# A decoder's second cross attention: steps of two key tiles and sums of exponentials on GpSimd

## The reference, cut to what matters

```
q = x @ Wq ; k = context @ Wk ; v = context @ Wv        # per head 1024x64, 6404x64, 6404x64
p = exp(q @ k.T / 8 - max)                              # softmax over the 6404 keys
o = (p @ v) / p.sum(-1)
y = x + concat(o) @ Wo + bo ; then a layer norm
```

## Time and profile before

| | us |
|---|---|
| median of 3 runs (lowest, highest) | 5546.07 (5544.38, 5546.73) |
| span of the profiled execution | 5512.1 |
| its own time beside the span | the runs' median is 34.0 above the span |
| busy: TensorE, VectorE, ScalarE, GpSimd | 4651.9, 3773.2, 2570.0, 866.4 |
| second cross attention, first K item to the last Y | about 2800 to 5386 |

### The profile page before, as it was taken

How to read it: one execution, slowest core, us unless ns; L and a number is a source line. 1 busy time by engine, 2 the same in 40 slices (tenths; PEclk the granted TensorE clock), 3 DMA queues, 4 the chain that set the end, 5 groups by cost and what they waited for, 6 DMA issues and landing times. The chain is left out here.

```text
span 5512.1 us, 68466 instructions
## 1 busy us (share of the span) xinstructions
PE 4651.9 (84%) x21823; PEld 2160.6 (39%) x21823; DVE 3773.2 (68%) x4226; ACT 2570.0 (47%) x4400; POOL 866.4 (16%) x798
## 2 busy tenths in 40 slices
PE   6898677767677777769969999999999999999993
PEld 2333343434343343423334444444444444444441
DVE  3666464737364655536648888888988888888865
ACT  1454463636363545515524555545555545545550
POOL 0000453625253544400010000000000000000000
PEclk6887798989898898968869999999999999999996
DMA  0000000000000000000000000000000000000000
GB/s 16 3 2 0 32 13 10 1 21 1 21 1 21 1 16 5 1 10 1 1 27 2 2 3 3 3 3 1 4 2 3 3 3 3 1 4 1 1 1 8
DMA packets 18039, 35.07 MB, mean 6 GB/s; under 512 B 3418, under 2 KB 12250, under 8 KB 16746
## 3 DMA queue, kind: packets, MB, share of 16 engines
q1 hardware_dynamic: 17642, 30.22, 1.7%
HBM read 29.69 MB, written 0.52 MB: 5 GB/s over the span
## 5 line engine op out<-in xcount | busy, mean ns | idle before, releaser
L1089 ACT ACTIVATE xat_p_full<-xat_sc 128x512 f32<-128x512 f32 (+1 forms) x1632 | 881.4, 593 | 677.4 <-PE xat_sc L1019 666.9
L1151 DVE TENSOR_REDUCE xat_part<-xat_ring 128x2 f32<-128x1024 f32 (+1 forms) x832 | 971.8, 1183 | 92.1 <-PE xat_ring L973 77.1
L1182 DVE TENSOR_TENSOR xat_p_sum<-xat_p_sum,xat_p_full 128x1024 f32<-128x1024 f32 x768 | 936.7, 1220 | 47.9 <-ACT xat_p_full L1089 40.4
L999 PE MATMUL xat_acc<-xat_p_full,xat_v 128*64 128x512 f32 (+1 forms) x3264 | 881.7, 618 | 2.5 <-ACT xat_o_raw L1094 2.5
L1018 PE MATMUL xat_sc<-xat_q_hh,xat_k_hl 128*128 128x512 f32 (+1 forms) x1632 | 785.6, 481 | 4.8 <-ACT xat_p_full L1089 4.7
L1019 PE MATMUL xat_sc<-xat_q_lm,xat_k_h 128*128 128x512 f32 (+1 forms) x1632 | 645.3, 395 | 0.0
L1018 PEld LDWEIGHTS xat_sc<-xat_q_hh,xat_k_hl 128*128 128x128 f32 (+1 forms) x1632 | 304.0, 186 | 497.9 <-ACT xat_p_full L1089 363.6
L1435 PE MATMUL loc_pr<-loc_w_qkv,loc_xs 128*128 128x512 f32 x576 | 364.8, 767 | 101.5 <-DVE loc_cosd L1703 56.0
L971 PE MATMUL xat_ring<-xat_k_hl,xat_q_hh 64*128 64x512 f32 (+1 forms) x832 | 387.6, 483 | 63.7 <-DVE xat_k_hl L1148 19.5
L1848 POOL PARTITION_ALL_REDUCE quant_top<-quant_part x5 | 1.8, 358 | 2681.9 <-DVE quant_part L1871 2681.9
L973 PE MATMUL xat_ring<-xat_k_up,xat_q_hh 64*128 64x512 f32 (+1 forms) x832 | 388.4, 484 | 0.0
(11 more groups left out here) (393 smaller groups left out, 7236.8 us busy)
## 6 DMA issues: line engine op xcount, KB each, us to landing
loc_w_qkv<-in_L_ffn_w SPq DMA_DIRECT2D x6, 1536.0 KB, 7.1
loc_w_o<-in_L_ffn_wo SPq DMA_DIRECT2D x6, 512.0 KB, 3.3
xat_ctxT<-in_ctxT SPq DMA_DIRECT2D x12, 256.0 KB, 2.7
xat_w_qk<-in_L_xattn_wqk SPq DMA_DIRECT2D x16, 128.0 KB, 2.4
loc_w<-in_L_ffn_w SPq DMA_DIRECT2D x6, 341.0 KB, 3.0
loc_w<-in_L_ffn_w SPq DMA_DIRECT2D x6, 192.0 KB, 2.3
loc_rope<-in_rope SPq DMA_DIRECT2D x1, 1024.0 KB
xat_w_o<-in_L_xattn_wo SPq DMA_DIRECT2D x16, 64.0 KB, 1.8
```

What stands on the lines that cost most here:

```text
L999: last = pe.matmul(acc[h * GROUP:(h + 1) * GROUP, :], v[0:size, t, e * GROUP:(e + 1) * GROUP], p_full[0:size, t % 3, cols(h)], start=(t == ...
L1089: act.activation(p_full[0:size, j % 3, cols(h)], sc[0:size, n % 3, :], ACT.Exp, scale=GROUP ** -0.5).then_inc(S["exp_done"], 1)
L1151: ins = dve.tensor_reduce(part[:, 2 * t:2 * t + 2, c], ring[:, b, :, 0:chunks[c][1]], AX.X, ALU.max)
L1182: dve.tensor_tensor(p_sum[:, e, :], first_in, p_full[:, (j - 1) % 3, :], ALU.add)\
```

## The change

A step is now two tiles (`pairs`, 26 steps, the last has the short tile alone), and both tiles are weighed one step later, one after the other. The sums move from VectorE to GpSimd, fold included, each add waiting for the one before. `p_full` has six buffers (`RING`) instead of three, used round through both heads (`buffer`). In a step with scores, three of the four halves are scored first, then K and V items, then the fourth half, then up to two M items, then the weighings; a third M item of a step comes after the weighings. ScalarE does Q's copy first, then the first tile's exponentials, then K's and V's copies, then the second tile's. The keys' order becomes 11, 0, 12, 1, 2 and on. K items stand at steps 1, 3 (the chunks 11 and 12) and 2, 4, 6 to 22; V at 3, 5 to 23 in odd heads and at 5, 7 and 9 in even ones; U after step 3, Y after step 5, T after the last.

```diff
-    order = [*range(OWN, NCH), *range(OWN)]
+    order = [OWN, 0, OWN + 1, *range(1, OWN)]
+    pairs = [range(j, min(j + 2, NT)) for j in range(0, NT, 2)]
+    NJ = len(pairs)
...
+    RING = 6
...
-            steps = [[[], [], []] for _ in range(NT if sums else NCH + 3)]
+            steps = [[[], [], []] for _ in range(NJ if sums else NCH + 3)]
...
-                last = 3 if sums else 0
-                steps[last + 1][post] += [("U", 0, 0)]
-                steps[last + 4][post] += [("Y", 0, 0)]
+                steps[3 if sums else 1][post] += [("U", 0, 0)]
+                steps[5 if sums else 4][post] += [("Y", 0, 0)]
...
-                for n, c in enumerate(order):
-                    steps[(2, 4)[n] if c >= OWN else PER * c + 5][pre] += [("K", c, 0)]
+                for c in order:
+                    steps[1 + 2 * (c - OWN) if c >= OWN else 2 * c + 2][pre] += [("K", c, 0)]
                 for n in range(NCH * NTOK // 2):
-                    steps[4 + n * 45 // (NCH * NTOK // 2)][mid] += [("M", order[n // 4], n % 4)]
-                steps[NT - 2][post] += [("T", 0, 0)]
+                    step = steps[2 + n * (NJ - 3) // (NCH * NTOK // 2)]
+                    step[mid if len(step[mid]) < 2 else post] += [("M", order[n // 4], n % 4)]
+                steps[NJ - 1][post] += [("T", 0, 0)]
...
-                at_step = min(v + 3, NCH + 1) if not sums else PER * v + 6 if v < V_EARLY else (3, 6, 9)[v - V_EARLY]
+                at_step = min(v + 3, NCH + 1) if not sums else 2 * v + 3 if v < V_EARLY else 2 * (v - V_EARLY) + 5
...
-        p_full = s.sb("p_full", [P, 3, T])
+        p_full = s.sb("p_full", [P, RING, T])
...
+                def score(n):
+
+                    j, h = divmod(n, 2)
+                    lo, size = tiles[j]
+                    lo = key_at(e, lo)
+                    if n >= 3 or part is not head_0:
+                        pe.wait_ge(S["exp_done"], at_.heads(2 * NT, n - 2))
+                    to = sc[0:size, n % 3, :]
+                    pe.matmul(to, k_hl[:, lo:lo + size], q_hh[:, e, cols(h)], start=True, stop=False)
+                    pe.matmul(to, k_h1[:, lo:lo + size], q_lm[:, e, cols(h)], start=False, stop=True)\
+                      .then_inc(S["s_ps"], 1)
+
                 for j, (pre, mid, post) in enumerate(part.steps):
+                    scores = [2 * t + h for t in pairs[j] for h in range(2)] if part.sums else []
                     for it in pre:
-                        item(*it)
...
+                        if it[1] == "Q" or not scores:
+                            item(*it)
...
+                    for n in scores[:3]:
+                        score(n)
+                    for it in pre:
+                        if it[1] != "Q" and scores:
+                            item(*it)
+                    for n in scores[3:]:
+                        score(n)
                     for it in mid:
                         item(*it)
                     if j == 0 and part.ends:
-                        weigh(NT - 1, prev, -NT)
+                        for t in pairs[-1]:
+                            weigh(t, prev, -NT)
...
-                        weigh(j - 1, e, 0)
+                        for t in pairs[j - 1]:
+                            weigh(t, e, 0)
...
+                def weights(t):
+
+                    size = tiles[t][1]
+                    if t >= RING or part is not head_0:
+                        act.wait_ge(S["pv_done"], at_.heads(NT, t - RING + 1))
+                        if t >= RING:
+                            act.wait_ge(S["sum_done"], at_.heads(N_SUM, max(1, t - RING)))
+                        elif t == RING - 1:
+                            act.wait_ge(S["fold_done"], at_.heads(1, 0))
+                        else:
+                            act.wait_ge(S["sum_done"], at_.heads(N_SUM, t - RING + 2))
...
                     if part.sums:
...
+                        for it in pre:
+                            if it[1] == "Q":
+                                fill(*it)
+                        weights(pairs[j][0])
+                    for it in pre:
+                        if it[1] != "Q" or not part.sums:
+                            fill(*it)
+                    if part.sums:
+                        for t in pairs[j][1:]:
+                            weights(t)
...
+            def body(at_):
+                if not at_.part.sums:
+                    return
+                e = at_.e
+                for t in range(1, NT - 1):
+                    pool.wait_ge(S["exp_done"], at_.heads(2 * NT, 2 * (t + 1)))
...
+                        pool.wait_ge(S["sum_done"], at_.heads(N_SUM, t - 1))
+                        first_in = p_sum[:, e, :]
+                    pool.tensor_tensor(p_sum[:, e, :], first_in, p_full[:, at_.buffer(t), :], ALU.add)\
+                        .then_inc(S["sum_done"], 1)
...
-                    if part_.sums and j >= 2:
-                        dve.wait_ge(S["exp_done"], at_.heads(2 * NT, 2 * j))
...
-                        dve.tensor_tensor(p_sum[:, e, :], first_in, p_full[:, (j - 1) % 3, :], ALU.add)\
-                           .then_inc(S["sum_done"], 1)
```

More of the change, by code:

```diff
@@ L867, in heads, with buffer @@
                 return at(self.i, 2 * per, self.head * per + c)
+            def buffer(self, t):
+                return (self.e * NT + t) % RING
             def shown(self, k):
@@ L999, in weigh @@
                         last = pe.matmul(acc[h * GROUP:(h + 1) * GROUP, :], v[0:size, t, e * GROUP:(e + 1) * GROUP],
-                                         p_full[0:size, t % 3, cols(h)], start=(t == 0), stop=(t == NT - 1),
-                                         skip_group_check=True)
+                                         p_full[0:size, (e * NT + t) % RING, cols(h)], start=(t == 0),
+                                         stop=(t == NT - 1), skip_group_check=True)
                     last.then_inc(S["pv_done"], 1)
+                def score(n):
[8 more added lines that the diff above has]
+                      .then_inc(S["s_ps"], 1)
@@ L1021, in body @@
+                    if part.sums and j == 0:
+                        pe.wait_ge(S["copy_done"], at_.heads(NCH, NCH))
+                        pe.wait_ge(S["ring_free"], at_.free(0))
+                    for n in scores[:3]:
[5 more added lines that the diff above has]
+                        score(n)
                     for it in mid:
@@ L1030, in body @@
                                        if part is not head_15 else (LOOPS + 1) * NV)
-                        if part is even and j == groups[V_EARLY][0] + 1:
+                        if part is even and groups[V_EARLY][0] in pairs[j - 1]:
                             pe.wait_ge(S["v_done"], at(at_.i, NV, 2 * NV))
-                        weigh(j - 1, e, 0)
+                        for t in pairs[j - 1]:
+                            weigh(t, e, 0)
                     for it in post:
@@ L1047, in body, with fill @@
                 hi = 0
+                def fill(l, kind, c, t):
+                    nonlocal hi
+                    b = (at_.n0 + l) % 2
+                    act.wait_ge(S["ring_ps"], at_.shown(l + 1))
+                    if kind == "Q":
+                        hi += 1
+                        act.activation(q_hh[:, nxt, :].rearrange("p (a b) -> p a b", a=2), ring[:, b, :, :],
+                                       ACT.Copy).then_inc(S["hi_done"], 1)
+                    elif kind == "K":
+                        hi += 1
+                        lo, width = chunks[c]
+                        lo = key_at(nxt, lo)
+                        act.activation(k_up[GROUP:P, order.index(c) % 3, 0:width], ring[GROUP:P, b, 0, 0:width],
+                                       ACT.Copy)
+                        act.activation(k_hl[0:GROUP, lo:lo + width], ring[0:GROUP, b, 0, 0:width], ACT.Copy)\
+                           .then_inc(S["hi_done"], 1)
+                        copies.append((lo, width, hi))
+                    elif kind == "V":
+                        if part is odd:
+                            act.wait_ge(S["pv_done"], at_.heads(NT, groups[c][-1] + 1))
+                        elif part is even:
+                            act.wait_ge(S["pv_done"], at_.heads(NT, 0))
+                        size, k = tiles[groups[c][0]][1], len(groups[c])
+                        act.activation(v[0:size, groups[c][0]:groups[c][0] + k, :],
+                                       ring[0:size, b, 0, 0:k * P].rearrange("p (t e) -> p t e", e=P), ACT.Copy)\
+                           .then_inc(S["v_done"], 1)
@@ new lines, in weights @@
+                def weights(t):
[8 more added lines that the diff above has]
+                            act.wait_ge(S["sum_done"], at_.heads(N_SUM, t - RING + 2))
+                    for h in range(2):
+                        n = 2 * t + h
+                        act.wait_ge(S["s_ps"], at_.heads(2 * NT, n + 1))
```

(25 more changed lines are left out.)

## The result

The changed kernel takes 5580.6 us (median of 4 runs, 5575.47 to 5582.32) against 5545.23 for the kernel before (4 runs). The ratio on record for these runs is 1.0083, 95% interval 1.0065 to 1.0101: slower by 0.8%, with no change outside the interval. The quotient of the two medians is 1.0064; one of the runs of before, 5520.55, lies 24 us under the other three. The forecast was 5625 (1.014), slower. The measured time lies 4 us under the forecast's own range (5585 to 5670) and inside the range for 8 in 10 (5500 to 5720).

A forecast was written before the change was run, and what follows sets the result against it. TensorE's stream, pausing at each change of kind, was taken as the bound. Heads with fills +76, head 0 +7.5 and head 15 +11 gave +95, 5641; another way gave 5607; the middle, 5625, was taken, range 5585 to 5670.

The forecast's parts named there:

- TensorE's distances are the bound, VectorE is not: Plain tile step of 2.57 us: TensorE's own distances set it, though VectorE needs 2.44 us of it.
- Merging saves the changes of kind: Scores and weighings of two tiles fall from 4.26 to 3.98 to 4.03 us; M items save another 3.4 a head.
- The rule on draining: A change of tiling mode drains TensorE; by this alone, two-tile steps halve the drains per tile and the kernel gets faster.
- The second M waits for K: Steps with K: the second M waits 1.50 us for K's buffer, +16.5 us a head over 11 steps.
- U's wait disappears: Behind U: the reciprocal's hold on the next M and V goes, as K waits anyway; 2.4 us saved a head.
- GpSimd is no bound except in head 15: GpSimd's adds at 2.43 us each fit within heads with fills; in head 15 they bound, +11 us.
- The sum: All heads: about +5.8 an odd and +5.1 an even one, +7.5 head 0, +11 head 15; total +95.
- The second way: Whole heads: if small unexplained waits hang on VectorE and go with its adds, 35 us go, giving 5607.
- The base: Whole kernel: profiled span 5512.1 us against a median of 5546.07, so 34.0 us added at the end.
- The signs: Trace marks: right if K steps take about 7.0 us and plain ones 4.7; wrong if 0.50 clock rows appear.
- The clock did fall: Rival, chance 0.10: TensorE's clock falls after idles in one K step in four, +70 us, 5695.
- GpSimd did hold VectorE: Rival, chance 0.07: GpSimd's adds hold up K's subtraction, mean wait 0.85 us in 180 K steps, +150, 5775.

The follow-up runs named there:

- e1: The kernel before with only the sums moved to GpSimd, with six buffers; ratio to before 0.9980.
- e5: The changed kernel with the second M behind the weighings in K steps, head 15's sums on VectorE and U behind the M items; 5344.2 us, ratio to before 0.9671.
- e3: The changed kernel with only one M item before the weighings in steps with a K item, the others behind them; 5394.08 us, ratio to before 0.9738.
- e2: The changed kernel with the sums and the fold back on VectorE, keeping pairs, order and six buffers; ratio to before 1.0149.
- e6: The changed kernel with K items before the three scores, for TensorE and ScalarE; ratio to before 0.9998.
- e8: The changed kernel with U's reciprocal written to PSUM, so the multiplication has one input in SBUF; ratio to before 1.0069.

## Why the prediction was right, and where it was off

- **TensorE's distances are the bound, VectorE is not.** Right: e1.
- **Merging saves the changes of kind.** Right in size: forecast 4.70 for a plain step, measured 4.61. Two weighings take 1.87 from the first to the next scores, forecast 1.93. That the pauses come from draining was not tested by itself. The rule on draining that I set beside it (the Trainium skill, "TensorEngine Tiling (Array Packing)", Tiling Modes) fits this trace, but by itself it gave the wrong sign for this kernel; in e5's order it would have given the right one.
- **The second M waits for K.** Right in place and mechanism: 3.15 forecast from K to M, 3.04 measured; 1.50 forecast for the wait, 1.38 measured; 11 steps a head. 11 x 1.38 x 15 heads is 228 us, and e3 gives back 189.5, with a new wait behind U in it.
- **U's wait disappears.** This step failed. I wrote that the K item waits there anyway and booked 2.4 us saved. But the two add up in VectorE's queue: reciprocal, multiplication, only then K's subtraction. An ordinary K step takes 6.84 us. The step behind U takes 8.00 at the clock of 1.00, 0.7 of the difference being the lock and the rest the queue, and where the clock falls some 1.7 more (9.67 above). Over 14 heads it takes 33 us more than ordinary K steps, half of that through the clock: the saving of 2.4 a head was about nothing. e2, e5 and e6 move this one place and the time follows.
- **GpSimd is no bound except in head 15.** Right, but mis-sized: +11 forecast. From T to U head 15 took 117.1 us before (5260.54 to 5377.60) and takes 132.85 now (5313.71 to 5446.56), +15.8. I took 2.43 from add to add; where each waits for the one before it is 2.54 (duration 2.37).
- **The sum.** Forecast for the stage +95 by one way and +61 by the other, taken +79; measured +56.3. Heads with fills: +3.3 an odd one and +1.7 an even one on the mean (7 each), head 0 +5.7. Part of the nearness is luck, since errors of both signs met. U's step was some 33 us too low and head 15 5 us. Against that the ordinary steps were too high: K steps came at 6.84 for a forecast of about 7.0, steps with V at 5.61 for 5.8, plain ones at 4.61 for 4.70, together some 50 us by my estimate from these rows. The second way, which let the small unexplained waits of before go away with VectorE's adds, was nearer; that they went for this reason isn't shown.
- **The base.** I added 34.0 us "around the span". That was wrong: in the changed kernel's profiled execution 2.3 us lie there (5582.32 against 5580.0). The profile of before was of an execution some 30 us shorter than the median of its runs, and its stage starts early among the traces (first item at 2797 us, 2793 to 2832 in all). Between the two profiles the span grew by 67.9 us, 13 of them before the stage; between the medians the time grew by 35, while the stage grew by 56. So some 20 us of the measured difference lie outside the stage or in the spread of the runs (5514.92 to 5552.52 for the same kernel in the later sets), and which isn't shown. The forecast had no term for it, and it too brought the total down.
- **The signs.** Most signs of being right came: the wait behind K, ended by VectorE's subtraction (3.04 us after K, for 3.1 to 3.2), steps near 7.0 and 4.7, GpSimd's adds as described. T to T was 154.7 and 165.6 on the mean instead of 157 and 167. One sign of being wrong came too: rows of 0.50 in the stage, in 11 heads.
- **The rivals.** The clock did fall, though behind U and not in ordinary K steps, whose idle is 1.11, and it cost about 17 us instead of 70. I also misread its record: I wrote that the clock fell after 3 of 14 pairs of waits behind U. In the trace of before it is granted 0.50 three times in the heads, but only the one at 4501.01 is behind U; those at 3692.05 and 4954.99 stand at a change of heads, 12 us before the step behind U. GpSimd did hold VectorE, but only the one operation with two inputs in SBUF. The Trainium skill, "SBUF — State Buffer", SBUF: two separate sides, says that such an operation and a GpSimd operation that reads SBUF exclude each other, and that the one that starts first holds the ports for its whole length. The traces agree: 0.69 us before, 1.37 with adds beside it, 0.69 again with one input in PSUM, while the subtraction stays at 0.69. In all 15 heads where an add was running, the multiplication ended 0.55 us after that add (above: add until 4225.92, multiplication until 4226.46). I had used that rule to dismiss the rival and overlooked the multiplication.

## What to carry to other kernels

Where items pass through a ring of two buffers, count for each item what stands between it and the item two places on; putting two consumers of the ring side by side can cost more than the merged steps save, and moving one of them behind a long piece of work costs little (0.2 us an item here). Before an engine is relieved, see at which places the bounding engine waits for it: here over 40% of VectorE's work in a head could go for 12 us in one order and for 66 us in another, and neither gain lay in the plain steps with one or two M items. Long operations that free a buffer (a reciprocal of 3.36 us) want their own place in the order, away from other short ones in the same queue.

## What the runs showed of the hardware

- VectorE's 128x512 multiplication with both inputs in SBUF took 0.69 us alone. Where one of GpSimd's adds was already running, it ended 0.55 us after the add: 1.32 to 1.47 us in the changed kernel, 2.77 to 2.88 behind U in e6. In heads 1 to 14 of e1 the two start within 0.1 us of each other: in three heads the multiplication took 2.90, in eleven 0.69, and the add then 2.8 to 2.9 instead of 2.37. With one input in PSUM the multiplication took 0.69 beside the same adds (e8). Its line of e1, in ns (minimum, median, maximum):

```profile
L1191 DVE TENSOR_TENSOR xat_o<-xat_o_raw,xat_inv x16: 691/692/2898, 3078.7 to 5390.9; 128x512 f32<-128x512 f32 x16
```

- A chain of dependent 128x1024 adds on GpSimd runs at 2.54 us each, 2.37 of it in the add; VectorE needs 1.22.
- After idles of 0.56 and 1.67 us with single M items between them TensorE's clock was granted 0.50 in 11 of 14 heads, for 3.41 us in ten and 6.83 in one. With idles of 1.11 us in the ordinary K steps it stayed at 1.00. It also stayed at 1.00 in all 14 heads of e3, with idles of 1.44 and 1.4 us in one step and K and one score between them.
